# Recommendation tower on one Trainium2 core: two loads of ids issued behind two tables, and ids on all 128 partitions

## The chip, the core and the metric

The kernel runs on one core of a Trainium2 chip. The core has five engines with queues of their own: PE (TensorE, matrix products), DVE (VectorE), ACT (ScalarE), POOL (GpSimd) and SP (SyncE, which here only issues DMAs). They meet through semaphores. The metric is the time of one execution in microseconds, the median of several runs.

## The reference

A batch of 2048 items. Each has a dense vector of 128 numbers and 26 ids; each id picks a row of 128 numbers from its table (1000 to 125000 rows). The 27 vectors of an item are multiplied with each other, and the 351 products go with the dense vector through three layers.

```
e = stack([tbl_f[ids[:, f]] for f in range(26)], axis=1)          # (2048, 26, 128)
combined = concatenate([dense[:, None, :], e], axis=1)            # (2048, 27, 128)
inter = einsum('bnd,bmd->bnm', combined, combined)[:, triu_i, triu_j]   # 351 pairs
h = concatenate([dense, inter, dense], axis=1)                    # 607 columns
h = maximum(h @ W_top1 + b_top1, 0)    # 512
h = maximum(h @ W_top2 + b_top2, 0)    # 256
y = h @ W_top3                         # 1
```

All of it is float32.

## The kernel before

The batch is cut into 16 tiles of 128 items; two tiles are a round (256 items, R = 256), and there are eight rounds. The 26 table lookups are done in two ways.

Seventeen features are gathered. POOL (`gather_tile`, L399) issues for each tile 17 indirect DMAs (L408) of 128 rows of 512 B into `rows[v % 2]`, two buffers that alternate by tile. Behind each gather POOL makes a `pause` (L390): a memset of a part of `y_wide` that nobody reads (L397). A tile's indices come by `load_idx` into `idx_sb`. The gathers of a tile form five groups, each with its semaphore; the dense rows (`load_dense`) are slot 0 of group 0. The last group holds two gathers. PE transposes group by group (`transpose_rows`, L429, its transposes at L443), and DVE and ACT copy the result into `vecs`. POOL may begin a tile when PE has transposed the tile two before (L402).

Nine features (`SPREAD`: eight tables of 1000 rows and one of 1250) are fetched with products on PE. At the start their tables are loaded as 125 partitions by 8 or 10 rows (`load_table`, L287, as two DMAs of 112 and 13 partitions), ACT casts each into `t_hi` (L673) and DVE makes the rest `t_lo` (L831). For each round the ids of these nine features are needed on 125 partitions, the same 256 ids on each. `load_ids` (L293) brings them, three features at a time, with a source that is one row broadcast over the partitions; three loads make a round, 25 loads in all. DVE (`compare`, L818) compares them with row numbers, which gives one-hot matrices, and PE (`fetch`, L472, matmuls at L483) multiplies these with `t_hi` and `t_lo`. The loads go to two buffers `ids_sb` that alternate; only the third load of the first round goes to `ids_first`, a part of `w2_sb` that is free at that time.

PE then makes the pair products (`dots`, L467), ACT and DVE move them into `inter` (L690, L866), ACT splits the input of the layers (L704), and `layer1` to `layer3` (L506, L515, L522) end a round. The order of the work on each engine is written out by hand: `step` for each round, `last_step` for the last. In the last step `stay_busy` (L570) has PE make transposes that nobody reads, while it is waiting.

SP issues all direct DMAs in one order, L308 to L353. The first loads are not held back by any wait: they go out one behind the other, as fast as SP can issue them. `load_ids` of later rounds waits for DVE's comparisons that read the buffer before (L300). At the start PE needs, for item k of the first round, table k in both parts and the comparisons of k: items 0 to 2 use the first load of ids, 3 to 5 the second, 6 to 8 the third. Behind items 1, 3, 4, 6 and 7 PE transposes the five groups of the first tile.

Of the kernel before, what the change touches and what calls it, by code (L numbers as in the profile page):

```python
# [5 lines left out]
P = 128  # L6
# [12 lines left out]
def dlrm_tower(nc, dense, ids, ids_by_round, tables, w1, w1_laid, w2, small_laid, out):  # L19
# [6 lines left out]
    R = 2 * P  # L26
# [30 lines left out]
    KP = 125  # L57
# [10 lines left out]
    NB = 3  # L68
# [3 lines left out]
    with ExitStack() as ctx:  # L72
# [55 lines left out]
        def split_count(n):  # L128
            return PIECES.index(n) + 1
# [7 lines left out]
        def staged_piece(n):  # L137
            if n < X:

                at = (n if n < 8 else (n - 8) * 2) * SIZE  # L140
                return vecs[1][:].rearrange("p t b n -> p (t b n)")[0:KP, at:at + KT[n] * D]
            if n == DENSE_W:
                return w_dense1
            return h1_sb[:].rearrange("p m r -> p (m r)")
# [62 lines left out]
        def groups_of(tiles):  # L207
            return (tiles + 2) * NG

        def static(i):  # L210
            return isinstance(i, int)
# [5 lines left out]
        def halves_made(i, r, k=0):  # L217
            return i * (2 * H) + (r + 1) * H + H0[k]
# [4 lines left out]
        def ids_place(r, k):  # L223
            return (r + 1 + k // NB) % 2

        def ids_count(i, r, k):

            before = (r + 1) * LOADS + k // NB
            return i * (LOADS * 16) + (before // 2 + 1 - (before > LOADS - 1 and before % 2 == 0)) * 16
# [31 lines left out]
        def passes(eng, step, last_step):  # L261
            step((0, 0), None)
            with eng.Fori(0, PASSES - 1) as i:
                step((i, 1), (i, 0))
                step((i + 1, 0), (i, 1))
            last_step(PASSES - 1)
# [11 lines left out]
        @block.sync  # L278
        def _(sp):
            def load_idx(i, v):  # L280
                sp.dma_start(idx[v][:], ids[bass.ds(i * (4 * P) + v * P, P), :]).then_inc(idx_in[v], 16)

            def load_dense(i, v):
                u = v % 2
                sp.dma_start(rows[u][:, 0, :], dense[bass.ds(i * (4 * P) + v * P, P), :]).then_inc(dense_in[u], 16)

            def load_table(n):  # L287

                src = tables[SPREAD[n] - 1].rearrange("(p t) d -> p (t d)", t=KT[n])
                for a, b in ((0, 112), (112, KP)):  # L290
                    sp.dma_start(staged_piece(n)[a:b], src[a:b]).then_inc(staged[n], 16)

            def load_ids(i, r, n, place=None):  # L293

                r, n = r + n // LOADS, n % LOADS
                if not (static(i) and i == 0 and r == -1):

                    done = (r * LOADS + n + LOADS - 2) // LOADS - 1
                    last = (n - 2) % LOADS * NB + NB
                    sp.wait_ge(compared, halves_made(i, done) + H0[last])  # L300
                if place is None:
                    place, filled = ids_sb[ids_place(r, n * NB)], ids_in[ids_place(r, n * NB)]
                else:
                    filled = ids_first_in
                src = ids_by_round[bass.ds(i * 2 + r + 1, 1), n * NB * R:(n + 1) * NB * R]
                sp.dma_start(place[0:KP].rearrange("p k n -> p (k n)"), src.to_broadcast([KP, NB * R])).then_inc(filled, 16)

            load_idx(0, 0)  # L308
            load_ids(0, -1, 0)
            load_table(0)  # L310
            load_table(1)
            load_ids(0, -1, 1)
            load_ids(0, -1, 2, ids_first)
            load_table(2)
            load_dense(0, 0)
            load_idx(0, 1)
            load_table(3)
            for n in range(4, 8):
                load_table(n)
            for n in range(8, X):  # L320

                sp.wait_ge(lo_made, split_count((n - 8) * 2 + 1))
                load_table(n)
            sp.dma_start(staged_piece(FIRST_W), w1_laid[:, 0:2 * H1]).then_inc(staged[FIRST_W], 16)
            load_dense(0, 1)
            load_idx(0, 2)
            load_idx(0, 3)
            load_ids(0, -1, 3)

            sp.wait_ge(compared, H)  # L330
            sp.dma_start(staged_piece(DENSE_W), w1_laid[:, 4 * H1:5 * H1]).then_inc(staged[DENSE_W], 16)
            sp.dma_start(w_dense2, w1[D + PAIRS:2 * D + PAIRS, :]).then_inc(dense_w_in, 16)
            sp.dma_start(small[:], small_laid[:, :]).then_inc(mlp_w_in, 16)
            load_ids(0, -1, 4)

            def load_last_w1():
                sp.wait_ge(lo_made, split_count(FIRST_W))
                sp.dma_start(staged_piece(LAST_W), w1_laid[:, 2 * H1:4 * H1]).then_inc(staged[LAST_W], 16)

            def load_w2():  # L340

                sp.wait_ge(lo_made, split_count(DENSE_W))
                sp.dma_start(w2_sb[:], w2.rearrange("(m p) n -> p m n", p=P)).then_inc(mlp_w_in, 16)

            def refill(i, v):
                sp.wait_ge(transposed, i * (4 * NG) + groups_of(v + 1))
                load_dense(*((i, v + 2) if v < 2 else (i + 1, v - 2)))
                load_idx(i + 1, v)

            def write_y(i, r):  # L350
                sp.wait_ge(y_kept, i * 2 + r + 1)
                sp.dma_start(out[bass.ds((i * 2 + r) * R, R), :].rearrange("t o -> o t"), y_sb[:, r, :]).then_inc(
                    out_written[r], 16)  # L353

            def step(now, prev):
                i, r = now

                load_ids(i, r, 2)
                refill(i, r * 2)
                load_ids(i, r, 3)  # L360
                if not prev:
                    load_last_w1()
                refill(i, r * 2 + 1)
                if not prev:
                    load_w2()
                load_ids(i, r, 4)
                if prev:
                    write_y(*prev)

            def last_step(i):  # L370
                write_y(i, 0)
                write_y(i, 1)


            for r in range(2):
                sp.sem_inc(out_written[r], 16)
            passes(sp, step, last_step)
            for r in range(2):
                sp.wait_ge(out_written[r], 16 + 16 * PASSES)

            for n in range(LOADS - 1):
                sp.wait_ge(ids_in[ids_place(1, n * NB)], ids_count(PASSES - 1, 1, n * NB))
            for v in range(2):
                sp.wait_ge(idx_in[v], 16 * (PASSES + 1))
# [637 lines left out]
```

## Time and profile before

| | before |
|---|---|
| time, median of 3 runs (lowest to highest) | 474.87 us (474.09 to 474.97) |
| profiled execution: its time | 477.4 us |
| profiled execution: span, first to last instruction | 475.4 us |
| mean granted clock of PE, as a share of full speed | 0.964 |
| busy PE, DVE, ACT, POOL | 416.0, 337.1, 214.8, 399.9 us |
| data moved by DMA | 36.58 MB |
| span at 40 slices, DMA share of slices 1 to 3 | 0.7, 0.9, 0.8 |

The profile is of one execution. Its time is 2.0 us over its span, which lies outside the first and the last instruction, and 2.5 us over the median of the runs without a profile. Times of rows count from the start of the span. Busy shares are averages over stages with different limits: at the start the DMA engines are full, later PE and POOL are.

### The profile page before, as it was taken

The page shows a single profiled execution, that of the slowest core. Times are in us where ns is not written, and L with a number is a line of the kernel's source. Part 1 is how long each engine was busy: PE and PEld are TensorE (multiplying, and loading weights), DVE is VectorE, ACT ScalarE, POOL GpSimd, SP SyncE. Part 2 cuts the span into 40 slices and gives each one's busy share as a digit, 9 for nine tenths or more (in the row PEclk, how much of TensorE's full clock was granted, in tenths as well). Part 3 has the DMA queues.
Part 4 walks back from the last instruction along what each step waited for, and adds up shares of the span by engine and source line. Part 5 has one row for each costly group of instructions (what it writes and reads, how often), then busy time and mean ns, then how long its engine had stood idle before and what let it go on. Part 6 is the DMA issues. An engine that isn't in the chain of part 4 may idle for free.

```text
span 475.4 us, 11713 instructions
## 1 busy us (share of the span) xinstructions
PE 416.0 (87%) x4210; PEld 391.8 (82%) x4210; DVE 337.1 (71%) x777; ACT 214.8 (45%) x719; POOL 399.9 (84%) x553
## 2 busy tenths in 40 slices
PE   0546786989999998999999989999699969989898
PEld 0436785989998998989898989999598969879786
DVE  3649878798698858786878769886588846844360
ACT  1044265454555344545544554555245453525352
POOL 7999999899899898998998989989989899899500
PEclk9978898889999999999999999999899998989999
DMA  7984413622221321323133313132132313121100
GB/s 174 219 206 128 114 43 79 160 65 71 72 78 42 79 80 46 78 72 85 41 79 76 80 42 83 48 84 65 40 84 73 79 45 79 44 74 41 29 2 0
DMA packets 19682, 36.58 MB, mean 77 GB/s; under 512 B 7823, under 2 KB 10391, under 8 KB 19630
## 3 DMA queue, kind: packets, MB, share of 16 engines
q0 software_dynamic: 8704, 17.84, 16.7%
q1 hardware_dynamic: 10926, 18.04, 13.3%
q8 instruction: 33, 0.54, 0.5%
q14 instruction: 19, 0.16, 0.1%
HBM read 35.85 MB, written 0.01 MB: 75 GB/s over the span
## 4 chain that ended last, share of the span: by engine, by line
POOL 61%; issue 25%; PE 8%; DMA 1%; POOLq 1%; DVE 1%; ACT 1%; DVEq 0%; ACTq 0%
POOL rows L408 34%; POOL y_wide L397 27%; PE dots_ps L467 2%; PE mlp_ps L506 2%; DMA rows<-in_tbl,idx_sb 1%; DVE inter L866 1%; POOLq L396 1%; PE late_ps L570 1%; PE mlp_ps L515 1%; PE turn_ps L548 1%; PE mlp_ps L557 1%; PE dots_ps L548 1%; ACT inter L690 1%; DMA idx_sb<-in_ids 0%; PE turn_ps L443 0%
## 5 line engine op out<-in xcount | busy, mean ns | idle before, releaser
L408 POOL DMA_INDIRECT rows<-in_tbl,idx_sb x272 | 265.9, 977 | 45.6 <-POOL y_wide L397 43.8
L818 DVE TENSOR_TENSOR onehot<-ids_sb,late_ps 125x1024 fp32r<-125x1024 int32 (+2 forms) x154 | 167.2, 1141 | 10.5 <-DMA ids_sb<-in_ids_by_round 6.5
L866 DVE COPY_PREDICATED inter<-mask,dots_ps 27x48 f32<-27x48 int32 x496 | 103.0, 208 | 79.1 <-ACT inter L690 62.6
L690 ACT COPY inter<-dots_ps 27x64 f32<-27x64 f32 x496 | 99.0, 200 | 92.4 <-PE dots_ps L467 58.7
L397 POOL MEMSET y_wide<- 64x448 f32 x272 | 133.9, 492 | 0.2
L467 PE MATMUL dots_ps<-vecs 128*64 128x54 f32 x1984 | 118.0, 225 | 1.9 <-issue 1.0
L467 PEld LDWEIGHTS dots_ps<-vecs 128*64 128x64 f32 x1984 | 114.0, 140 | 6.5 <-issue 3.4
L483 PE MATMUL turn_ps<-onehot,t_hi 125*128 125x256 f32 x378 | 100.5, 302 | 11.4 <-DVE vecs L646 11.4
L483 PE MATMUL turn_ps<-onehot,t_lo 125*128 125x256 f32 x378 | 96.0, 291 | 0.0
L483 PEld LDWEIGHTS turn_ps<-onehot,t_hi 125*128 125x128 f32 x378 | 75.2, 199 | 15.8 <-issue 10.0
L483 PE MATMUL late_ps<-onehot,t_hi 125*128 125x256 f32 x214 | 60.1, 314 | 22.1 <-DVE t_lo L831 17.2
L483 PEld LDWEIGHTS turn_ps<-onehot,t_lo 125*128 125x128 f32 x378 | 75.5, 200 | 0.2
L483 PEld LDWEIGHTS late_ps<-onehot,t_hi 125*128 125x128 f32 x214 | 44.6, 209 | 25.6 <-DVE t_lo L831 18.7
L483 PE MATMUL late_ps<-onehot,t_lo 125*128 125x256 f32 x214 | 57.0, 299 | 0.0
L666 ACT COPY vecs<-turn_ps 128x256 f32<-128x256 f32 x46 | 28.5, 620 | 60.5 <-PE turn_ps L483 55.4
L483 PEld LDWEIGHTS late_ps<-onehot,t_lo 125*128 125x128 f32 x214 | 44.7, 209 | 0.1
L443 PE MATMUL turn_ps<-ident,rows 128*128 128x128 f32 x200 | 30.2, 279 | 16.0 <-DMA rows<-in_tbl,idx_sb 8.0
L443 PEld LDWEIGHTS turn_ps<-ident,rows 128*128 128x128 f32 x200 | 22.6, 142 | 18.4 <-DMA rows<-in_tbl,idx_sb 8.9
L506 PE MATMUL mlp_ps<-x_hi,w_hi 128*128 128x256 f32 x140 | 35.9, 291 | 0.0
L506 PE MATMUL mlp_ps<-x_hi,w_lo 128*128 128x256 f32 x140 | 34.7, 283 | 0.0
L666 ACT COPY vecs<-late_ps 128x256 f32<-128x256 f32 x26 | 16.1, 620 | 32.3 <-PE late_ps L483 29.5
L646 DVE COPY vecs<-turn_ps 128x512 f32<-128x512 f32 (+1 forms) x28 | 17.7, 637 | 16.3 <-PE turn_ps L443 15.6
(84 smaller groups left out, 364.2 us busy)
## 6 DMA issues: line engine op xcount, KB each, us to landing
ids_sb<-in_ids_by_round SPq DMA_DIRECT2D x25, 375.0 KB
rows<-in_tbl,idx_sb POOLq DMA_INDIRECT x272
vecs<-in_tbl SPq DMA_DIRECT2D x8, 448.0 KB
rows<-in_r_dense_features SPq DMA_DIRECT2D x16, 64.0 KB
h_sb<-in_W_top_laid SPq DMA_DIRECT2D x2, 512.0 KB
vecs<-in_tbl SPq DMA_DIRECT2D x1, 560.0 KB
w_sb<-in_W_top SPq DMA_DIRECT2D x1, 512.0 KB
vecs<-in_tbl SPq DMA_DIRECT2D x8, 52.0 KB
```

The costliest lines, as they stand in the source:

```text
L397: pool.memset(unread, 0.0).then_inc(pauses_made, 1)
L408: nc.gpsimd.indirect_dma_start(out=rows[v % 2][:, s, :], out_offset=None, in_=tables[f - 1][:, :], in_offset=bass.IndirectOffsetOnAxis(ap= ...
L443: last = pe.transpose(bank[:, n * P:(n + 1) * P], rows[u][:, s, :], ident[:])
L467: last = pe.matmul(place[h * 64:h * 64 + 64, n, 0:PAIR], vs[:, b:b + 2, :].rearrange("p b f -> p (b f)"), vs[:, b:b + 2, 0:N], start=True, ...
L483: last = pe.matmul(bank, part[0:KP, T0[k] + t, :], part_buffer(k, h)[0:KP, t - a, :], start=(t == 0 and part is t_hi), stop=(t == KT[k] - ...
L506: last = pe.matmul(mlp_ps[m % 2], w[:, jj, m * P:(m + 1) * P], x[:, jj, :], start=(at == 0), stop=(at == 3 * (JG + 1) - 1))
L548: last = pe.matmul(end_ps[m], w[:, jj, m * P:(m + 1) * P], x[:, jj, :], start=False, stop=(at == 3 * JG - 1))
L646: copy(vecs[v // 2][:, v % 2, :, a:a + n], bank_of("rows", i * 4 + v, k)[:, 0:n * P].rearrange("p (f b) -> p b f", f=n)).then_inc(done, 1)
L666: nc.scalar.copy(vecs[(r + 1) % 2][:, :, :, NR + k], bank_of("item", i * 2 + r + 1, k)[:, 0:R].rearrange("p (t b) -> p t b", t=2)).then_in ...
L690: nc.scalar.copy(inter_of(u, q, g, 0, count[g]), products_of(q, g * JG, count[g], place)).then_inc(inter_by_act, 1)
L818: dve.tensor_tensor(part_buffer(k, h)[0:KP, 0:n], home.rearrange("p (o r) -> p o r", o=1).to_broadcast([KP, n, R]), row_of[KT[k]][0:KP, a: ...
L866: dve.copy_predicated(inter_of(u, q, g, a, n), mask[g * 32:g * 32 + N, a:a + n].rearrange("p (j s) -> p j s", s=1).to_broadcast([N, n, QS] ...
```

## The change

SP issues the first loads in another order. The second load of ids goes behind the third table (`load_table(2)`), the third load behind the fourth (`load_table(3)`); the dense rows of the first tile come between the second load of ids and the fourth table. The number of DMAs is the same. And every load of ids, 25 in all, fills 128 partitions and not 125 (`KP`); DVE and PE still read 125.

```diff
@@ load_ids
-                sp.dma_start(place[0:KP].rearrange("p k n -> p (k n)"), src.to_broadcast([KP, NB * R])).then_inc(filled, 16)
+                sp.dma_start(place[:].rearrange("p k n -> p (k n)"), src.to_broadcast([P, NB * R])).then_inc(filled, 16)
@@ block.sync
             load_idx(0, 0)
             load_ids(0, -1, 0)
             load_table(0)
             load_table(1)
+            load_table(2)
             load_ids(0, -1, 1)
+            load_dense(0, 0)
+            load_table(3)
             load_ids(0, -1, 2, ids_first)
-            load_table(2)
-            load_dense(0, 0)
             load_idx(0, 1)
-            load_table(3)
             for n in range(4, 8):
                 load_table(n)
```

## Rows read from the trace of the kernel before

**Rows 1.** The page: busy time by engine, and the last chain's shares.
```profile
PE 416.0 (87%) x4210; PEld 391.8 (82%) x4210; DVE 337.1 (71%) x777; ACT 214.8 (45%) x719; POOL 399.9 (84%) x553
...
POOL 61%; issue 25%; PE 8%; DMA 1%; POOLq 1%; DVE 1%; ACT 1%; DVEq 0%; ACTq 0%
```

**Rows 2.** The page's groups: form, count, busy us, mean ns, idle before, releaser.
```profile
L408 POOL DMA_INDIRECT rows<-in_tbl,idx_sb x272 | 265.9, 977 | 45.6 <-POOL y_wide L397 43.8
...
L397 POOL MEMSET y_wide<- 64x448 f32 x272 | 133.9, 492 | 0.2
```

**Rows 3.** POOL's waits over the span: total us, times, longest.
```profile
POOL rows L408 <- DMA idx_sb<-in_ids: 1.9, 1, 1.9
```

**Rows 4.** POOL's gathers in order of time: start us, duration us, instruction.
```profile
3.59 1.14 POOL L408 DMA_INDIRECT rows<-in_tbl,idx_sb  x1 [1.86 <-DMA idx_sb<-in_ids]
...
15.02 2.42 POOL L408 DMA_INDIRECT rows<-in_tbl,idx_sb  x1 [0.16 <-POOL y_wide L397]
...
60.62 0.95 POOL L408 DMA_INDIRECT rows<-in_tbl,idx_sb  x1 [0.16 <-POOL y_wide L397]
...
117.62 0.95 POOL L408 DMA_INDIRECT rows<-in_tbl,idx_sb  x1 [0.16 <-POOL y_wide L397]
...
389.92 1.09 POOL L408 DMA_INDIRECT rows<-in_tbl,idx_sb  x1 [0.16 <-POOL y_wide L397]
...
415.70 0.95 POOL L408 DMA_INDIRECT rows<-in_tbl,idx_sb  x1 [0.16 <-POOL y_wide L397]
...
417.31 1.18 POOL L408 DMA_INDIRECT rows<-in_tbl,idx_sb  x1 [0.16 <-POOL y_wide L397]
...
443.17 1.25 POOL L408 DMA_INDIRECT rows<-in_tbl,idx_sb  x1 [0.16 <-POOL y_wide L397]
...
445.07 0.95 POOL L408 DMA_INDIRECT rows<-in_tbl,idx_sb  x1 [0.16 <-POOL y_wide L397]
```

**Rows 5.** PE's transposes of a last group, and PE's idle time before.
```profile
76.35 0.38 PE L443 MATMUL late_ps<-ident,rows 128*128 128x128 f32 x2
...
110.86 0.41 PE L443 MATMUL late_ps<-ident,rows 128*128 128x128 f32 x2
...
337.86 0.44 PE L443 MATMUL turn_ps<-ident,rows 128*128 128x128 f32 x2 [2.61 <-DMA rows<-in_tbl,idx_sb]
...
392.55 0.44 PE L443 MATMUL late_ps<-ident,rows 128*128 128x128 f32 x2 [2.19 <-DMA rows<-in_tbl,idx_sb]
...
422.37 0.44 PE L443 MATMUL turn_ps<-ident,rows 128*128 128x128 f32 x2 [1.93 <-DMA rows<-in_tbl,idx_sb]
```

**Rows 6.** The chain that ended last, from 422 us on: start us, us, what.
```profile
422.81 2.29 PE mlp_ps L506 x15
425.11 4.67 PE dots_ps L467 x64
429.78 3.78 PE mlp_ps L506 x30
433.56 3.68 PE dots_ps L467 x64
...
450.12 0.22 PE turn_ps L443 x2
```

**Rows 7.** Windows: from:to, us, busy by engine (count), PE's granted clock, DMA share, GB/s.
```profile
12.00:33.00 21.00, 8.34 (x42) 7.79 (x43) 11.07 (x16) 4.71 (x5) 19.05 (x25) 0.88 1.04 221
418.00:422.00 4.00, 2.44 (x21) 2.06 (x20) 3.45 (x5) 1.63 (x3) 3.68 (x6) 1.00 0.48 130
420.00:421.00 1.00, 0.44 (x5) 0.20 (x2) 1.00 (x3) 0.58 (x1) 0.84 (x3) 1.00 0.58 186
424.00:426.00 2.00, 2.00 (x15) 1.78 (x14) 0.00 (x0) 0.47 (x1) 1.84 (x3) 0.50 0.25 66
```

**Rows 8.** SP's queue: the last load of ids.
```profile
416.94 0.28 SPq L306 DMA_DIRECT2D ids_sb<-in_ids_by_round  x1
```

**Rows 9.** ACT in order of time: the cast of the third table.
```profile
28.67 1.04 ACT L673 CAST t_hi<-vecs 125x1024 fp32r<-125x1024 f32 x1 [15.12 <-DMA vecs<-in_tbl]
```

## The prediction

> **What bounds the kernel now.** The page comes first. PE is busy for 416 of 475.4 us and looks like the bound, but the chain that ended last spends 61% of the span on POOL [rows 1]. The table of groups says with what: 272 gathers of 977 ns and as many pauses of 492 ns [rows 2]. The list of waits shows that POOL waits for nobody else: 1.9 us for the first indices, then only for its own pauses, never for PE to free a rows buffer [rows 3]. POOL's timeline gives the beat: most gathers last 0.95 us and follow each other every 1.60 us (415.70 and 417.31 are such a pair). The first is issued at 3.59 and the last at 445.07 [rows 4]. 271 beats of 1.60 are 434; the real distance is 441.5, so some 7 us are gathers that took longer than 0.95. The same comes out of the group: 265.9 less 272 x 0.95 is 7.5 us [rows 2]. Most of it is early: the 69th gather, the first of the fifth tile, starts at 117.62, 114.0 us after the first, where 68 beats of 1.603 make 109.0. The largest single one is the eighth gather, 2.42 us at 15.02 [rows 4].
>
> PE starts late and catches up. The last gather of the second tile is issued at 60.62, and PE transposes it only at 76.35 [rows 4, 5]. The first time PE waits for a gather is just before 337.86; from then on it is tied to POOL at tile ends [rows 5]. So whatever PE gains before some 330 us is worth nothing at the end: it only waits earlier for the same gathers.
>
> The end is the place to look at. A last gather of a tile normally serves PE 2.6 us after its start (389.92 to 392.55) [rows 4, 5]. That of tile 15 of 16, started at 417.31, serves it only at 422.37, 5.06 us later, after PE has been idle for 1.93 us, since 420.44 [rows 4, 5]. From there the chain is PE, then ACT and DVE, without a gap until the end; the last tile's last gather, of 445.07, is taken at 450.12 with no wait [rows 6]. Beside the late gather stands a load of ids, issued by SP at 416.94 [rows 8]. The windows show it as DMA traffic of 130 GB/s from 418 to 422, with 186 in the third of these four us, where 424 to 426 has 66 [rows 7]. And PE pays twice: in 424 to 426 the granted clock is 0.50, the lower level of 1.2 GHz [rows 7], and 64 dots take 4.67 us instead of 3.68 [rows 6].
>
> **Part 1, ids on 128 partitions.** Nothing is computed with the three new rows, so DVE's 154 comparisons stay as they are. Each of 25 loads grows from 375 to 384 KB, 2.4%. What can change is how a load is divided over the 16 DMA engines; the timeline doesn't show that directly. What it shows is 520 KB in the four us from 418 to 422, which are the load's 375 and two gathers of 64: the load has 94 to 125 GB/s for itself if it takes 4 to 3 us, while the mixed traffic of the start runs at 221 GB/s [rows 7]. That a load uses only a part of the engines would explain both.
>
> The Trainium skill says this outright (DMA: Bandwidth & Descriptors, Why a DMA increments its semaphore by 16 and not by 1): a DMA runs on the largest number up to 16 that divides the slowest dimension, which is 5 for 125 partitions and 16 for 128. By its 27 GiB/s per engine, an estimate from that page, a load would take 2.65 us before and 0.85 after. The same section has a semaphore's increment land only after all earlier writes of its engine, across queues, which would hold a gather back until its five engines are through with the ids. The trace agrees: the gather lands when the load's traffic ends, near 422.
>
> In the tail, with the load spread: it begins to move at about 418.6, and 384 KB at 221 GB/s (start-up) to 186 GB/s (the collision itself) are 1.7 to 2.1 us, so it is over at 420.3 to 420.7 with the gather inside it. A clean landing would be 417.31 + 2.63 = 419.94. PE is ready at 420.44. So its idle time shrinks from 1.93 to between 0 and 0.3. Without it I expect the clock to stay up; the low stretch costs about 1.0 us on the dots (4.67 - 3.68) and 0.4 on the 15 matmuls before them (2.29, where 30 take 3.78) [rows 6]. That makes PE 1.9 + 1.4 = 3.3 us earlier. What is late next is the last gather of all: 445.07 + 2.63 = 447.7, and PE would be there at 450.12 - 3.3 = 446.8 and wait. The gain is capped at 450.12 - 447.7 = 2.4 us. Ends: 0 (the gather lands as late as now) and 2.4; I take 2.2, near the cap, since 1.9 alone already comes from the idle time.
>
> In the loop the other loads aren't felt by PE's end. POOL feels some: in six cases, from 154 us on, a gather begins 0.3 to 0.45 us after a load's issue and lasts 1.06 to 1.18 instead of 0.95 (416.94 with 417.31 is the last) [rows 4, 8], about 1.0 us in all. The gather of 443.17 takes 1.25 with no load near it [rows 4], so I leave this at nothing, with ends -1.0 (all six vanish) and +1.0 (they double).
>
> **Part 2, the order of the first loads.** Thirteen issues keep their number; SP only issues them in another order, between 3.3 and 7.5 us. Passed are the third table (earlier by two ids loads), the dense rows, the fourth table and the second tile's indices. Now ACT has converted the second table by 13.55 and waits 15.1 us for the third, until 28.67 [rows 9], since both ids loads, 750 KB, are ahead of it; PE is busy for only 8.3 of the 21 us from 12 to 33 [rows 7]. With the third table ahead of them it should land one table (512 KB, 2.3 us at 221 GB/s) after the second, which was there by 12.5: near 15. The ids that items 3 to 5 need are then behind 512 KB less. The prologue on PE should end 10 to 18 us earlier. All of that lies under POOL, and PE's wait for gathers merely moves from 337 to an earlier tile. I count 0 for it. If that cover weren't there it would be 10 us or more. The indices of the second tile are first needed by POOL at its 18th gather (3.59 + 17 x 1.60 + 1.5, about 32), and stay among the first 3.2 MB, which at 221 GB/s take 15 us and have passed by about 17: no wait.
>
> What reaches POOL is the eighth gather's extra of 2.42 - 0.95 = 1.47 us at 15.02 [rows 4], in the midst of a DMA share of 1.04 [rows 7]. It may come from gathers held up behind ids on a few engines, and then it goes; or from the total traffic, and then it stays, since the bytes are the same. Ends: -1.5 and +0.5 (a third of itself on top, as the full DMA engines then serve the same bytes). The traces don't decide; I take half, -0.7.
>
> **Sum.** -2.2 - 0.7 = -2.9 us on the profiled execution, 477.4 to 474.5. Its 477.4 stands 2.5 over the median of 474.87; the difference carries over: 472.0.
>
> **Rivals.** (a) More than I count: the early extras of POOL, 5.0 us before 117.62 (114.0 - 109.0) [rows 4], go for the most part, by 3, with the crowded engines. Then -2.4 - 3: 469.5. For: all that follows up to 445.07 has only some 2 us of them. Against: the whole first 110 us run at a far lower traffic than 12 to 33, and the extras aren't only in that stretch (5.0 against the 1.5 of the eighth gather). Chance 0.13. (b) No change: the load is spread over all engines, so that now every part of the gather is behind it, and it lands at 422 as before; or the clock falls anyway and a new idle stretch of PE at 447 takes the gain back. 474.5. For: 16 engines busy with ids leave no free one; against: the load is over by 420.7. Chance 0.22. (c) The change doesn't do what it says: 128 rows are divided as 125 are, and the order is hidden by POOL. 474.9. The 94 to 125 GB/s of a load speak against it. Chance 0.07. (d) Slower: a load on all 16 engines delays POOL's next gather each time. With 25 loads at 0.23 us, the largest extra beside one now, less the 1.0 already paid, that is +4.8, or 477.5 with the gain in the tail. It decides from 0.12 us more per load on (25 x 0.12 = 2.9). For: six such extras now; against: with the DMA engines full from 12 to 33 us [rows 7] only the eighth gather stands out. Chance 0.08. A second way to be slower I rule out: POOL waits for PE only if the third tile is transposed after 117.62, where the fifth begins to be gathered into its place; it is done at 111.3 now, 6.3 us ahead [rows 4, 5], and the start gets earlier.
>
> The Trainium skill has a rule that leans to (b) and (d) (DMA: Bandwidth & Descriptors, Issuing engines are not separate DMA queues): transfers of SP and GpSimd run on the same 16 engines and interleave. By it alone a spread load meets every gather on every engine. The 3 to 4 us that one load takes now say that the meeting gets shorter.
>
> **Numbers.** Forecast 0.50, at 472.0 with 470.5 to 473.2 of its own; (a) 0.13, (b) 0.22, (c) 0.07, (d) 0.08. What a measurement of this kernel can tell from no change is 0.2%, 0.95 us, so faster means below 473.9: (a), nearly all of the forecast and a little of (b), 0.66; the same 0.25; slower 0.09. The range from 469.6 to 475.3 takes in (a) to (c) and leaves out (d).
>
> **What would show it.** Right: ACT's third conversion near 15 to 17 instead of 28.67; PE's first wait for a gather well before 337; the last gather of tile 15 served within 3.2 us; no granted clock of 0.50 at 424; first to last gather 440.8 us apart or less. The term of the tail is wrong if PE still idles over 1 us at about 420 (or wherever that load now falls: if DVE's earlier work moves the load away from the gather, the gain is the same for another reason). The start is wrong if the eighth gather still takes over 2 us. All of it is wrong if any gather of POOL waits for PE, or if the beat of 1.60 us changes.

## The result

The changed kernel takes 473.49 us (472.41 to 474.86, 13 runs) against 474.45 us (473.68 to 475.48, 13 runs) of the kernel before: a ratio of 0.9975, with a 95% interval of 0.9965 to 0.9985. That is about 1.0 to 1.2 us less, where 2.4 to 2.9 had been forecast. Of all executions reported here one, the slowest of e7's six, was in a slower state with a lower clock and is left out of its median. The profiled execution of the changed kernel has a span of 472.2 us and a time of 473.94, close to its median. The one of before had 475.4 and 477.4, which is 3 us above its median of 474.45. That difference turned out to matter most.

The profile after, first the page's groups for POOL (form, count, busy us, mean ns, idle before), which answer to [rows 2]:

```profile
L408 POOL DMA_INDIRECT rows<-in_tbl,idx_sb x272 | 264.6, 973 | 45.6 <-POOL y_wide L397 43.7
...
L397 POOL MEMSET y_wide<- 64x448 f32 x272 | 134.0, 493 | 0.2
```

POOL's timeline after (start, duration), with the rows that answer to [rows 4]: the first gather, the long one (now the seventh), the last of the 15th tile, and the last of all.

```profile
3.64 1.14 POOL L408 DMA_INDIRECT rows<-in_tbl,idx_sb  x1 [1.90 <-DMA idx_sb<-in_ids]
...
13.48 2.42 POOL L408 DMA_INDIRECT rows<-in_tbl,idx_sb  x1 [0.16 <-POOL y_wide L397]
...
416.81 0.95 POOL L408 DMA_INDIRECT rows<-in_tbl,idx_sb  x1 [0.16 <-POOL y_wide L397]
...
444.13 0.95 POOL L408 DMA_INDIRECT rows<-in_tbl,idx_sb  x1 [0.16 <-POOL y_wide L397]
```

PE's transposes after, with the idle time before them: the second tile's last group, the first wait for a gather, a late one, and the last group of all, as in [rows 5].

```profile
68.35 0.38 PE L443 MATMUL late_ps<-ident,rows 128*128 128x128 f32 x2
...
173.02 0.44 PE L443 MATMUL turn_ps<-ident,rows 128*128 128x128 f32 x2 [0.47 <-DMA rows<-in_tbl,idx_sb]
...
392.08 0.44 PE L443 MATMUL late_ps<-ident,rows 128*128 128x128 f32 x2 [2.62 <-DMA rows<-in_tbl,idx_sb]
...
446.70 0.44 PE L443 MATMUL turn_ps<-ident,rows 128*128 128x128 f32 x2 [0.38 <-DMA rows<-in_tbl,idx_sb]
```

The chain that ended last, after: it runs through POOL to the very last gather, and only then through PE.

```profile
444.13 2.52 DMA rows<-in_tbl,idx_sb
446.65 0.04 issue
446.70 0.44 PE turn_ps L443 x2
```

Two windows after (from:to, us, busy by engine, granted clock, DMA share, GB/s), as in [rows 7], and ACT's cast of the third table, as in [rows 9]:

```profile
12.00:33.00 21.00, 14.21 (x92) 13.54 (x92) 19.20 (x21) 10.81 (x14) 19.06 (x25) 1.00 1.04 262
...
424.00:426.00 2.00, 2.00 (x37) 1.94 (x34) 0.37 (x2) 1.26 (x7) 1.84 (x4) 1.00 0.12 33
```

```profile
13.39 1.04 ACT L673 CAST t_hi<-vecs 125x1024 fp32r<-125x1024 f32 x1 [1.77 <-DMA vecs<-in_tbl]
```

The two profiles differ by 3.2 us of span, and by the forecast's own terms: the low clock at 424 us is gone, and the end comes 28.1 us after the last gather (472.2 - 444.13) and not 30.3 (475.4 - 445.07), which is the 2.2 of the tail; POOL's distance from first to last gather shrinks from 441.5 to 440.5. Had this pair been all there is, the forecast would look right. The medians say otherwise, so the question was which of the two is the kernel.

### The profile page after: what moved, and what is told of

The parts are those of the page before. It is cut to its first block, busy times and chain, and to the rows that moved or that the text cites. A ratio compares the mean times of both kernels' runs of the same rounds, so it can differ in the third digit from the quotient of the medians.

```text
span 472.2 us, 11713 instructions
## 1 busy us (share of the span) xinstructions
PE 419.5 (89%) x4210; PEld 395.2 (84%) x4210; DVE 338.9 (72%) x777; ACT 216.5 (46%) x719; POOL 398.9 (84%) x553
## 4 chain that ended last, share of the span: by engine, by line
POOL 65%; issue 28%; PE 3%; POOLq 1%; DVE 1%; DMA 1%; ACT 1%; DVEq 0%; ACTq 0%
POOL rows L408 36%; POOL y_wide L397 29%; POOLq L396 1%; DVE inter L866 1%; PE turn_ps L548 1%; PE mlp_ps L557 1%; PE dots_ps L548 1%; ACT inter L690 1%; DMA rows<-in_tbl,idx_sb 1%; PE dots_ps L467 0%; DMA idx_sb<-in_ids 0%; PE turn_ps L563 0%; ACT x_hi L704 0%; ACT rows L796 0%; PE turn_ps L443 0%
## 5 line engine op out<-in xcount | busy, mean ns | idle before, releaser
L467 PE MATMUL dots_ps<-vecs 128*64 128x54 f32 x1984 | 120.1, 227 | 1.5 <-ACT vecs L666 0.9
L467 PEld LDWEIGHTS dots_ps<-vecs 128*64 128x64 f32 x1984 | 116.2, 142 | 6.2 <-issue 2.8
L483 PE MATMUL turn_ps<-onehot,t_hi 125*128 125x256 f32 x378 | 103.6, 309 | 11.0 <-DVE vecs L646 10.4
L483 PE MATMUL turn_ps<-onehot,t_lo 125*128 125x256 f32 x378 | 98.9, 296 | 0.0
L483 PEld LDWEIGHTS turn_ps<-onehot,t_hi 125*128 125x128 f32 x378 | 77.5, 205 | 15.7 <-issue 8.3
L483 PEld LDWEIGHTS turn_ps<-onehot,t_lo 125*128 125x128 f32 x378 | 77.8, 206 | 0.2
L483 PE MATMUL late_ps<-onehot,t_hi 125*128 125x256 f32 x214 | 57.6, 305 | 18.8 <-DVE t_lo L831 15.9
L483 PEld LDWEIGHTS late_ps<-onehot,t_hi 125*128 125x128 f32 x214 | 42.8, 200 | 21.6 <-DVE t_lo L831 16.2
L483 PE MATMUL late_ps<-onehot,t_lo 125*128 125x256 f32 x214 | 54.7, 291 | 0.0
L483 PEld LDWEIGHTS late_ps<-onehot,t_lo 125*128 125x128 f32 x214 | 43.0, 201 | 0.1
L443 PE MATMUL turn_ps<-ident,rows 128*128 128x128 f32 x200 | 31.2, 284 | 12.1 <-DMA rows<-in_tbl,idx_sb 12.1
L646 DVE COPY vecs<-turn_ps 128x512 f32<-128x512 f32 (+1 forms) x28 | 17.9, 640 | 27.8 <-PE turn_ps L443 27.7
```

Of the source, the lines that this page charges most:

```text
L443: last = pe.transpose(bank[:, n * P:(n + 1) * P], rows[u][:, s, :], ident[:])
L467: last = pe.matmul(place[h * 64:h * 64 + 64, n, 0:PAIR], vs[:, b:b + 2, :].rearrange("p b f -> p (b f)"), vs[:, b:b + 2, 0:N], start=True, ...
L483: last = pe.matmul(bank, part[0:KP, T0[k] + t, :], part_buffer(k, h)[0:KP, t - a, :], start=(t == 0 and part is t_hi), stop=(t == KT[k] - ...
L646: copy(vecs[v // 2][:, v % 2, :, a:a + n], bank_of("rows", i * 4 + v, k)[:, 0:n * P].rearrange("p (f b) -> p b f", f=n)).then_inc(done, 1)
```

## Experiments

Of each run the table has median and ratio, and three things read from its profile. The distance is from POOL's first gather to its last. The extras are what gathers take over 0.95 us, added up over the timeline, in three stretches. The tail is the span less the start of the last gather. Ratios are against runs of the kernel before on the same chip, whose medians are 474.65 us for e1 to e4, 475.25 for e5 to e8 and 474.74 for e9 to e12. Distance, extras and tail are of one profiled execution each.

| run | median us | ratio (95%) | distance | extras to 60, 60 to 110, after 110 us | tail |
|---|---|---|---|---|---|
| before, first profile | 474.45 | | 441.5 | 4.1, 0.9, 2.2 | 30.3 |
| changed, first profile | 473.49 | 0.9975 (0.9965 to 0.9985) | 440.5 | 4.1, 0.5, 0.8 | 28.1 |
| e1 before again | 474.90 | 0.9994 (0.9980 to 1.0007) | 441.8 | 3.5, 1.5, 2.2 | 28.1 |
| e2 order only | 474.72 | 0.9997 (0.9981 to 1.0013) | 440.6 | 4.4, 1.1, 0.5 | 28.2 |
| e3 width only | 473.41 | 0.9965 (0.9952 to 0.9978) | 439.9 | 3.3, 1.6, 0.5 | 28.1 |
| e4 changed again | 473.51 | 0.9976 (0.9959 to 0.9993) | 439.5 | 3.2, 1.3, 0.7 | 28.0 |
| e5 before, one SBUF input | 469.28 | 0.9868 (0.9841 to 0.9895) | 435.8 | 0.2, 0.1, 0.3 | 31.2 |
| e6 changed, one SBUF input | 468.95 | 0.9861 (0.9834 to 0.9888) | 435.5 | 0.2, 0.0, 0.3 | 28.0 |
| e9 before, no last load | 474.67 | 0.9994 (0.9979 to 1.0008) | 441.9 | 3.3, 1.3, 2.7 | 28.1 |
| e10 first three loads wide | 473.69 | 0.9980 (0.9964 to 0.9996) | 440.3 | 3.8, 0.8, 0.9 | 28.0 |
| e11 changed, high part in PSUM | 470.39 | 0.9906 (0.9883 to 0.9930) | 436.6 | 0.2, 1.4, 0.8 | 27.8 |
| e12 before, high part in PSUM | 471.57 | 0.9927 (0.9904 to 0.9950) | 439.0 | 0.8, 1.1, 2.5 | 27.9 |

### Is the first profile of before typical? (e1, e4)

e1 is the kernel before and e4 the changed kernel, both without an edit.

> The kernel before, unchanged, profiled once more. Theory A (the tail is as the first profile shows it in every execution): the last gather of the 15th tile again serves PE about 5.0 us after its start, PE's granted clock falls to 0.50 behind it, the last tile's last group is transposed 5.0 us after its gather, and the span is near 475.4 us. Theory B (the first profile of before was an unlucky execution, some 3 us above its own median of 474.45): the tail comes out differently, most of the 5.06 us wait or the low clock stretch is missing, and the span is 472 to 473 us, so that the 2.4 us that the tail was to give were never there in the median. POOL's extras over 0.95 us (7 us in all) should be at the same places in both theories for the first 60 us.

Measured: span 473.4 in the profile, median 474.90. PE waits only 0.90 us at the end of the 15th tile, the granted clock stays at 1.00 from 424 to 426, and it is the last gather of all that PE waits for. PE's transposes of last groups in e1, and that window:

```profile
422.79 0.44 PE L443 MATMUL turn_ps<-ident,rows 128*128 128x128 f32 x2 [0.90 <-DMA rows<-in_tbl,idx_sb]
...
447.85 0.44 PE L443 MATMUL turn_ps<-ident,rows 128*128 128x128 f32 x2 [0.17 <-DMA rows<-in_tbl,idx_sb]
```

```profile
424.00:426.00 2.00, 2.00 (x27) 1.87 (x26) 0.00 (x0) 0.47 (x1) 1.75 (x3) 1.00 0.12 33
```

PE's first products of `layer2` behind it, in the first profile of before and in e1:

```profile
442.06 1.97 PE L515 MATMUL mlp_ps<-h_sb,w_sb 128*128 128x256 f32 x8 [1.57 <-ACT h_sb L711]
```

```profile
439.62 1.97 PE L515 MATMUL mlp_ps<-h_sb,w_sb 128*128 128x256 f32 x8 [0.22 <-ACT h_sb L711]
```

The gather of the 15th tile is late here too (started at 418.05, it serves at 422.79, 4.74 us later). But it costs PE 0.9 us and no clock, and PE still reaches the last group in time for the last gather of 445.33. So the mishap of the first profile lies behind the late gather, and it has two parts. From the last group of the 15th tile to the next transposes (422.37 to 437.17, against 422.79 to 436.09 in e1) PE takes 1.5 us more, with the low clock; and before `layer2` it waits 1.57 us for ACT and not 0.22. Why ACT was later there is not settled. Of the 75 executions of the kernel before in these experiments (e1's 12 and the 63 beside the experiments), half have spans between 472.4 and 473.4, and one is over 474.3, at 476.0. The first profile, with 475.4, was as rare an execution. Theory B holds.

> The changed kernel once more on the same chip as the other three: ratio 0.9975 again (0.9965 to 0.9985). Its tail: the last gather decides (4.13 to 6.70 in the last digits of its first profile, 2.57 us), no granted clock of 0.50 after 420 us. If the two profiles of this kernel differ by more than 1 us in their spans, single profiles can't carry a sum of 3 us.

The changed kernel repeats: 0.9976, and the last gather decides (tail 28.0). Its two profiles differ by 1.2 us in the span, which is the size of the whole effect: single profiles of this kernel can't carry a sum of 3 us.

### Which half of the change does it? (e2, e3, e10)

e2 keeps 125 partitions and takes the new order; e3 keeps the old order and takes this line alone:

```diff
-                sp.dma_start(place[0:KP].rearrange("p k n -> p (k n)"), src.to_broadcast([KP, NB * R])).then_inc(filled, 16)
+                sp.dma_start(place[:].rearrange("p k n -> p (k n)"), src.to_broadcast([P, NB * R])).then_inc(filled, 16)
```

> Only the order of the first loads is changed; ids stay on 125 partitions. If the order is hidden under POOL, as predicted: within 0.5 us of before, although PE's prologue ends several us earlier (third conversion by ACT well before 28.67 us). If the gain is from the order, through POOL's collisions with DVE in a loop whose phase has moved: about -1 us. On engines: if 125 partitions go over 5 DMA engines, the loads that stay narrow still hold up the tables, and the third conversion is later than the 13.39 us of the changed kernel.

> Only the width: ids on 128 partitions in every load, the old order. If the width alone spreads the loads over all engines: first comparison by DVE at about 6.3 us as in the changed kernel and not 7.9, the third conversion well before 28.67 though two loads of ids are still ahead of the third table (750 KB more at 221 to 250 GB/s: about 3 us later than the changed kernel's 13.39, so 16 to 17). If the gain is from the width (tail, or loads that end sooner): -1 us or more; if not: within 0.5 us of before.

Measured: the order alone gives nothing (0.9997), the width alone all of it (0.9965). The third table is converted by ACT at these times with the order alone, and with the width alone:

```profile
14.49 1.04 ACT L673 CAST t_hi<-vecs 125x1024 fp32r<-125x1024 f32 x1 [1.37 <-DMA vecs<-in_tbl]
```

```profile
15.91 1.04 ACT L673 CAST t_hi<-vecs 125x1024 fp32r<-125x1024 f32 x1 [4.68 <-DMA vecs<-in_tbl]
```

With 125 partitions and two loads of ids ahead of it the third table came at 28.67 [rows 9]; with 128 and the same two loads ahead it comes at 15.91, 12.8 us earlier. The Trainium skill's account of it (DMA: Bandwidth & Descriptors, Why a DMA increments its semaphore by 16 and not by 1), 5 engines for 125 and 16 for 128, agrees with these times. The packet records of the traces show the same for every load: of a narrow load of the loop in before never more than 8 packets overlap in time, of a wide one in after 14 to 20 at the most. One load of the loop in each, beside gathers: the narrow one issued at 205.69 in before moves from 206.6 to 211.0, 4.4 us, the wide one issued at 206.81 in after from 207.8 to 209.9, 2.1 us. Over all loads of the loop in these two profiles it is 3.1 to 4.5 us against 1.9 to 3.3. A window in that load of before, and one around that of after:

```profile
207.00:210.50 3.50, 3.50 (x32) 3.36 (x31) 2.60 (x4) 1.55 (x4) 3.17 (x6) 1.00 0.53 137
```

```profile
207.50:210.00 2.50, 2.50 (x24) 2.50 (x23) 2.17 (x11) 2.20 (x9) 2.34 (x3) 1.00 0.78 237
```

e10 widens only the three loads of the start:

```diff
+                first = static(i) and i == 0 and r == -1
+                rows_filled = P if first else KP
-                sp.dma_start(place[0:KP]..., src.to_broadcast([KP, NB * R]))
+                sp.dma_start(place[0:rows_filled]..., src.to_broadcast([rows_filled, NB * R]))
```

> The kernel before, ids on 128 partitions in the first three loads only; the 22 later loads stay on 125. Theory C (what the width moves is when the prologue ends, and with it which gathers of POOL meet DVE's splits): the whole gain of the width is here, -1.0 to -1.3 us. If instead the loads of the loop or of the tail are what matters: within 0.3 us of before.

Measured: 473.69, 0.9980 (0.9964 to 0.9996), 1.05 us less. The 22 loads of the loop may stay narrow; most of the gain is with the first three (1.05 us here, 1.24 in e3, with intervals that overlap). So the gain is, in the main, not a transfer of the loop or of the tail that got quicker. It is something that an earlier start changes, while POOL, which sets the time, starts at the same moment: PE transposes the last group of the second tile at 66.8 us in e10 and at 66.6 in e3, against 76.35 in before. In e2, which gains nothing, it does so at 70.95.

### The last load (e9)

SP's order is written out for it, and one load is left out:

```diff
+                if now != (PASSES - 1, 0):
+                    load_ids(i, r, 4)
-                load_ids(i, r, 4)
...
-            passes(sp, step, last_step)
+            written_out(step, last_step)
```

> The kernel before without its last load of ids, the one that SP issues at 417 us beside the last gather of the 15th tile; nobody reads what it brings. If that load costs the typical execution its end (my term of 2.2 us): near -2 us in the median, and the gather serves PE within 2.7 us. If the end is set by the last gather of all in a typical execution (first to last instruction = last gather + 28.1 us): within 0.5 us of before, and only the few executions above 475.5 us go.

Measured: 474.67, 0.9994: nothing. In the profile the gather of the 15th tile (417.94) is served at 421.47, after 3.5 us and without a wait of PE for it, where it took 4.7 in e1. So the load does seem to have held the gather back, but the load of 416.94 us on which my largest term rested costs the typical execution nothing.

### What makes gathers long (e5, e6)

In the traces nearly every long gather begins while DVE is in a split, a subtraction of two tensors of SBUF, the core's main memory (L831 for tables and weights, L875 and L883 for the layers' input). Of the gathers of 1.00 us or more it is 20 of 22 in the first profile of before and 13 of 15 in that of the changed kernel; the others are the very first and the one of 2.42 us. DVE's and POOL's timelines of the changed kernel around some of them:

```profile
13.92 2.29 DVE L831 TENSOR_TENSOR t_lo<-vecs,t_hi 125x1024 fp32r<-125x1024 f32 x2
...
30.28 1.22 DVE L831 TENSOR_TENSOR t_lo<-vecs,t_hi 125x1024 fp32r<-125x1024 f32 x1
...
34.28 1.22 DVE L831 TENSOR_TENSOR t_lo<-vecs,t_hi 125x1024 fp32r<-125x1024 f32 x1
```

```profile
29.59 0.95 POOL L408 DMA_INDIRECT rows<-in_tbl,idx_sb  x1 [0.16 <-POOL y_wide L397]
31.20 1.13 POOL L408 DMA_INDIRECT rows<-in_tbl,idx_sb  x1 [0.16 <-POOL y_wide L397]
34.59 1.74 POOL L408 DMA_INDIRECT rows<-in_tbl,idx_sb  x1 [0.16 <-POOL y_wide L397]
```

The gather of 34.59 starts 0.91 us before its split ends and is 0.79 too long; that of 31.20 starts 0.30 before and is 0.18 too long. That of 29.59 starts 0.69 us before a split begins and is a normal one. The longest, of 13.48, doesn't fit this: it starts 0.44 us before two splits in a row and is held up all the same, until 15.90. The gather of 417.31 in before, which I had put down to the load of ids, has this beside it on DVE:

```profile
416.99 0.68 DVE L883 TENSOR_TENSOR x_lo<-inter,x_hi 128x512 fp32r<-128x512 f32 x1
```

The split ends 0.36 us after the gather's start, and the gather is 0.23 too long. The load stood beside it only because SP issues it when DVE has passed the same point. e5 and e6 take the second SBUF input away from the splits, L875 and L883 in the same way as L831, in all but the last step: the other operand is a row number in PSUM, the memory that PE writes its products to. These two kernels leave out the true low parts.

```diff
-                dve.tensor_tensor(piece(n, False), staged_piece(n), piece(n, True).bitcast(F32),
-                                  ALU.subtract).then_inc(lo_made, 1)
+                dve.tensor_tensor(piece(n, False)..., staged_piece(n)...,
+                                  row_of[KT[n]][0:KP]...to_broadcast([KP, KT[n], D]),
+                                  ALU.subtract).then_inc(lo_made, 1)
```

> The kernel before, but DVE's splits (L831, L875, L883, all but those of the last step) subtract row numbers that lie in PSUM where they subtracted the high part from SBUF, so that each has only one input from SBUF; the low parts are wrong by that, and everything else is computed. Theory C (POOL's gathers of over 0.95 us are those begun while DVE subtracts two tensors of SBUF): the eighth gather drops from 2.42 to 0.95 us, all extras together from 7.2 to under 1 us, the last gather is issued 434.5 to 436 us after the first (441.5 and 441.8 now), and the time falls by 5 to 6.5 us. Theory D (the extras come from DMA traffic or from the loads of ids): the eighth gather stays near 2.4 us and the time within 1 us.

> The changed kernel with the same edit (low parts wrong in the same way). Theory C: it falls by less than the kernel before does, since it has fewer extras left (5.4 and 5.2 us against 7.2), and the two kernels come out within 0.5 us of each other: all that the change gave were fewer meetings of gathers and splits. If the wide loads give something else too (tail, DMA), this one stays about 1 us under the other. Theory D: both fall by nothing.

Measured: 469.28 and 468.95. The extras fall from 7.2 to 0.6 us in e5 and from 5.2 to 0.6 in e6, and the distance to 435.8 and 435.5, where 271 beats of 1.603 are 434.4. DVE's split in e5 lasts as long as before, at the same place, and the gather in it is a normal one (DVE, then POOL):

```profile
15.45 2.29 DVE L832 TENSOR_TENSOR t_lo<-vecs,late_ps 125x1024 fp32r<-125x1024 f32 x2
```

```profile
15.01 0.95 POOL L408 DMA_INDIRECT rows<-in_tbl,idx_sb  x1 [0.16 <-POOL y_wide L397]
```

In e5 21 gathers begin inside such a split with more than 0.15 us of it left and take 0.95 or 0.96; one meets a split of the last step, which still has both operands in SBUF, and takes 1.06. So it is the second input from SBUF that delays a gather's issue, not DVE being busy and not DMA traffic: the loads, tables and gathers are the same in e5. The gather of 2.42 us goes with it too, so the splits are needed for it; why it was held up from before they began is open. Without these meetings the two kernels are 0.3 us apart where they were 1.0 to 1.2. So most of the gain of the change came by way of these meetings; whether the 0.3 is anything at all, these runs don't settle (e5's executions take 468.95 to 472.56 us, e6's 468.28 to 469.54).

The Trainium skill has the mechanism (SBUF — State Buffer, Who interferes with whom): a DVE instruction with two inputs in SBUF contends with a GpSimd instruction that reads SBUF, as one read port is common to both. The extras agree with it; the page's remark that tensor_tensor didn't stall a DMA in the probe it tells of doesn't hold for the indirect gather here, which was held up by 0.79 us at 34.59.

e5's profiled execution has a tail of 31.2 us. Its clock is at 1.00 up to 434 us; then PE is idle for 2.34 us, up to 435.57, before `layer2` (L515), and the profile names nothing that it waits for; the clock is at 0.50 from 436 to 438. It is the slowest of its seven executions (span 470.6, the others 467.1 to 467.8). The tail can go wrong in more than one way.

### A version that keeps the result (e11, e12)

For eight tables ACT writes the high part once more, into the two layer banks of PSUM, and DVE reads it there, in two halves:

```diff
                 nc.scalar.copy(piece(n, True), staged_piece(n)).then_inc(hi_made, 1)
+                if n < 8:
+                    if n:
+                        act.wait_ge(lo_made, n)
+                    for m in range(2):
+                        nc.scalar.copy(mlp_banks[m][0:KP, :].bitcast(F32R), staged_piece(n)[:, m * 512:(m + 1) * 512]).then_inc(hi_in_psum, 1)
...
+                    for m in range(2):
+                        dve.wait_ge(hi_in_psum, 2 * n + m + 1)
+                        part = slice(m * 512, (m + 1) * 512)
+                        last = dve.tensor_tensor(piece(n, False)[:, part], staged_piece(n)[:, part], mlp_banks[m][0:KP, :], ALU.subtract)
+                    last.then_inc(lo_made, 1)
```

> The changed kernel; for the first eight tables ACT writes the high part a second time, into the two layer banks of PSUM that are free in the prologue, and DVE subtracts that, in two halves of 512, so that these splits have one input from SBUF. Theory C: the extras of POOL before 60 us fall from 3.2 to 4.1 us to under 1 (the ninth table, the weights and the loop keep theirs), -2.5 to -3.5 us against the changed kernel, so 470 to 471. Against it: 16 more ACT copies in the prologue, some 9 us of ACT's idle time, may make PE late, which the beat should cover.

> The kernel before with the same edit as e11_after_psum. Theory C: -2.5 to -3.5 us against before. If the change's own gain lies in the loop's meetings (2.2 us of extras after 110 us before, 0.5 to 0.8 after), this stays 1 us or more above e11_after_psum; if it lies in the prologue's, the two come out equal.

Measured: 470.39 and 471.57, 3.1 us below the changed kernel of e4 (on another chip) and 3.2 below before (474.74). Both are as theory C had it. The seventh gather, of 2.42 us at 13.48 in the changed kernel, is normal in e11, with all the table traffic around it:

```profile
13.42 0.95 POOL L410 DMA_INDIRECT rows<-in_tbl,idx_sb  x1 [0.16 <-POOL y_wide L399]
```

And the 1.2 us between e11 and e12 are the change's gain, still there with the prologue's extras nearly gone from both. That points to the loop, where e12 has 2.5 us of extras after 110 us and e11 has 0.8. It is one profile of each, though, and the two are 2.5 us apart in time where the medians are 1.2 apart: e12's is the slowest of its six executions. e11 is the fastest version with the full result, 0.9906 of before.

### Does POOL's beat cover the rest? (e7, e8)

POOL's pause is cut from 448 to 384 columns, in before and in the changed kernel:

```diff
-        unread = y_wide[64:P, 0:448]
+        unread = y_wide[64:P, 0:384]
```

> The kernel before with POOL's pause cut from 448 to 384 columns, so the beat is 1.60 - 0.07 = 1.53 us, 18 us less over 271 beats. If POOL's beat is all that bounds the kernel (the cover of my sum): up to -18 us. If PE is close behind: PE, 13 us late at the second tile, doesn't catch up in time any more, and the gain is a few us only, or POOL begins to wait for PE to free rows.

> The changed kernel with the same shorter pause. If the cover by POOL hid the change's earlier start (PE has the second tile at 68.35 instead of 76.35), it shows here: 4 to 8 us below the kernel before with the short pause. If PE's start is hidden by something else as well, the two differ by 1 us as they do now.

Measured: 548.52 and 540.12 us, ratios 1.1502 (1.1455 to 1.1550) and 1.1386 (1.1347 to 1.1425). A kernel 15% slower was in none of my expectations. The beat is 1.55 us in e7, but now POOL does wait for PE at the tiles' ends, which I had named as possible (five steps of 9.5 to 12.6 us), and PE is busy for 449.6 us and not 416.0 and stands idle inside `dots`. The idle time before L467 by releaser, in before and in e7:

```profile
  issue: 4.3, 9
```

```profile
  issue: 54.0, 142
```

"issue" is idle time without a cause that the profile shows, and the 54.0 adds up two things that overlap, 20.8 us before matmuls (61 times) and 33.2 before their weight loads. So why PE stalls there when gathers come 0.05 us closer was not settled, nor what makes up the 73 us. What the pair does show is the cover: with POOL no longer the bound, the changed kernel is ahead of before by 8.4 us in the medians and by 5.5 in the ratios, about what I had expected (4 to 8). Its PE has the last group of the second tile at 68.46 and not at 77.28.

## Why the prediction was wrong, point by point

- **The base of the sum.** "The difference carries over: 472.0" is the step that failed. I made the sum on an execution that stood 2.5 us above the median of three runs, and took this for the price of profiling. The changed kernel's profile stood 0.45 above its median, e1's 0.2. Most of the 2.5 was an accident of that execution, at the very place where I found the largest term.
- **The tail, -2.2.** The mechanism is in the pair of profiles to the tenth: 30.3 to 28.1 us behind the last gather, clock at 1.00, the last gather as the new cap. That fit comes from the cap; what the cap hid was priced wrong. I had put PE's delay at 1.9 of idle time and 1.4 of clock; against e1 the clock took 1.5, and a wait of PE for ACT of 1.57 us at 442.06 (0.22 in e1), which my sum doesn't have, as much again. In the typical execution of before the cap holds already (e1: tail 28.1), and leaving out the accused load changes nothing (e9: 0.9994). The term is 0, and not -2.2.
- **The start, -0.7.** Wrong in cause and size; the term is 0. The long gather of 2.42 us is in e1 to e4 as it was, wide or narrow, early or late; e5 and e11 remove it by the splits' operand. I had offered ids on a few engines, or the total traffic, and never laid DVE's timeline beside POOL's.
- **The loop's extras, 0 with ends of -1.0 and +1.0.** This is where the profiles put the gain: 2.2 us after 110 us in before and e1, 0.8 and 0.7 in the two profiles of after, 1.4 less. That it is so in the median as well is argued, not shown, since e2 has only 0.5 there and gains nothing. I had the rows (six gathers beside six loads), blamed the loads, and put the sign at even.
- **Part 1, the load is spread.** Right: start-up traffic from 12 to 33 us rises from 221 to 262 GB/s, and a load of the loop takes 1.9 to 3.3 us and not 3.1 to 4.5. That is longer in both than the 0.85 and 2.65 us that I had estimated from the Trainium skill's figure per engine; the measured times hold. What I cited for increments across queues stands in another section of that page of the Trainium skill (DMA: Bandwidth & Descriptors, Queues, rings and completion order).
- **Part 2, order.** Third table near 15: 13.39. PE's first wait for a gather moves to 173 from 337 (280 in e1), and POOL hides it all: e2 is 0.9997. Right, though PE's start moved by less than the 10 to 18 us forecast (second tile at 68.35 and 66.53 in the two profiles, against 76.35), and the price of 10 us or more without the cover was of the right kind (5.5 to 8.4 us in e7 and e8). One sentence was a slip: the second and third load of ids have more in front of them in the new order, not 512 KB less.
- **The signs named.** No wait of POOL for PE (one of 0.2 us is put down to PE in e4, no longer than the pause before every gather), the beat unchanged, no low clock at 424, 440.8 us or less between the gathers: met. The last gather of tile 15 served within 3.2 us: met in the first profile, missed in e4 (415.51 to 419.45). And the sign that the start is wrong came: the long gather still takes 2.42 us. The signs of the tail test the profile against the profile, so they could not catch the wrong base.
- **Rivals.** What came nearest is (b), no change at 474.5, though for another reason. The range of 469.6 to 475.3 was meant to take in (a) and leaves out its 469.5. The gain of 1 us fits no rival; the chance of which gathers meet a split was not among them.

What stays open: why the order alone doesn't move the median, though its profile has only 0.5 us of extras after 110 us (that execution was 0.8 us below its own median, and the spans of e2 reach from 470.6 to 474.1). A start that is earlier changes which gathers meet a split, but no run predicts which way; e2, e3, e4 and e10 all start earlier, and only the wide ones gain. The start of e2 is earlier by 5.4 us at the second tile, that of the others by 8.0 to 9.8, and no run tells whether that is the difference.

## What to carry to other kernels

Before a sum is made on a profiled execution, compare its span with the spans of other executions: where it stands 0.5% above them, what looks like the largest stall may be what is special about it. When an instruction of one engine now and then takes longer than its kind, lay the other engines' timelines beside it and look for what is always there at that moment, above all DVE beside POOL. And a change that only shifts two engines' work against each other can be worth a few tenths of a per cent, here 0.25%; removing what collides (here 3 us by an operand in PSUM) was worth more than moving it.

## What the hardware showed that I had not expected

- A GpSimd indirect gather whose issue takes 0.95 us takes longer when it starts while DVE is subtracting two tensors of SBUF. What it is held up by is the rest of the split less 0.12 us (0.91 left, 0.79 too long; 0.36 left, 0.23 too long; 0.30 left, 0.18 too long). A split that begins after the gather leaves it alone (29.59), with the one of 2.42 us as the exception. With one of the operands in PSUM the same subtraction, equally long, costs a gather nothing.
- A pause of 384 and not 448 columns between gathers, 0.05 us of beat, made the kernel 15% slower, with PE idle in `dots` for 20.8 us, in 61 pieces, before matmuls that wait for nothing that the profile shows. The cause is open.
- PE's granted clock went to half speed behind an idle time of 1.93 us in one execution of before and stayed up behind 0.90 us in another. That was 1.5 of the 2.9 us that PE then took longer to the last group; a wait for ACT was the rest.
